# A linear-attention and expert-ffn layer on one core: the own-token term moved onto the diagonal of the attention matrix, the output gated from PSUM, a new order of the slot's tail

## What is computed

```python
x = x + _layernorm(attn(_layernorm(x)))
x = x + _layernorm(ffn(_layernorm(x)))
# attn: 4 heads, 64 key and 128 value features a head
S = jnp.exp(gt)[:, None] * S + kt[:, None] * vt[None, :]   # step over tokens
o = qt @ S
o = o * lax.rsqrt(mean(o * o, -1) + EPS) * rms_w           # per head
o = o.reshape(b, t, DV) * silu(x @ Wg)
return o @ Wo
# ffn: 8 experts, two sequences each
h = gelu(tokens @ w1 + b1); y = h @ w2 + b2
```

## Time and profile before

| | us |
|---|---|
| median of 3 runs | 1318.27 (1318.04 to 1319.22) |
| the profiled execution, its own time | 1316.67 |
| its span, first to last instruction | 1314.9 |
| TensorE busy | 1245.6 (95%) |
| VectorE busy | 1035.5 (79%) |
| ScalarE busy | 711.3 (54%) |
| GpSimd busy | 637.5 (48%) |

### The profile page before, as it was taken

One profiled execution on the slowest core, in us unless ns is written; L12 is line 12 of the kernel. 1 busy time (PEld: TensorE's weight loads), 2 busy tenths in 40 slices (PEclk: granted clock), 3 DMA queues, 4 the chain that ended last, 5 costly groups with the idle time before them and its releaser, 6 DMA issues. The chain is left out here.

```text
span 1314.9 us, 23430 instructions
## 1 busy us (share of the span) xinstructions
PE 1245.6 (95%) x8388; PEld 1096.4 (83%) x8388; DVE 1035.5 (79%) x2404; ACT 711.3 (54%) x1427; POOL 637.5 (48%) x889
## 2 busy tenths in 40 slices
PE   5889999999999999999999999999999999999957
PEld 3778889888898888889888888988889888898956
DVE  4769788796978969788787978879787796978863
ACT  5365555655456465654756555565545646465423
POOL 5436453563445544564435644356354554456431
PEclk9989999999999999999999999999999999999988
DMA  2110010100101001010011001010010100100000
GB/s 97 37 33 17 17 49 1 53 17 17 49 21 48 3 17 49 22 49 2 17 49 53 16 17 47 3 53 16 17 49 18 44 9 17 49 21 33 1 17 16
DMA packets 31778, 38.27 MB, mean 29 GB/s; under 512 B 2448, under 2 KB 29104, under 8 KB 31664
## 3 DMA queue, kind: packets, MB, share of 16 engines
q1 hardware_dynamic: 31136, 36.25, 8.3%
q10 hardware_dynamic: 528, 0.52, 0.1%
HBM read 28.38 MB, written 8.39 MB: 28 GB/s over the span
## 5 line engine op out<-in xcount | busy, mean ns | idle before, releaser
L1041 POOL TENSOR_TENSOR k_decayed<-k_decayed,block_totals 128x256 f32<-128x256 f32 x192 | 170.4, 887 | 248.3 <-PE ps_level L304 248.0
L304 PE MATMUL ps_level<-q_blockdiag,k_decayed 128*128 128x128 f32 x1792 | 263.9, 282 | 13.2 <-DVE q_blockdiag L586 12.5
L304 PEld LDWEIGHTS ps_level<-q_blockdiag,k_decayed 128*128 128x128 f32 x1792 | 234.9, 191 | 34.9 <-DVE q_blockdiag L586 24.6
L576 DVE COPY_PREDICATED attn_T<-level_masks,ps_level 128x512 f32<-128x512 uint32 x160 | 153.1, 957 | 21.6 <-PE ps_level L304 21.4
L1047 POOL TENSOR_TENSOR rstd<-rstd,minus_half 128x1 f32<-128x1 f32 x192 | 111.7, 584 | 106.5 <-DVE rstd L638 106.5
L586 DVE TENSOR_TENSOR q_blockdiag<-q_blockdiag,block_totals 128x512 f32<-128x512 f32 x192 | 140.0, 730 | 27.3 <-PE ps_level L304 27.2
L261 PE MATMUL ps_big<-w_ff_hi,h_hi 128*128 128x256 f32 x512 | 150.0, 293 | 2.5 <-DVE h_lo L591 2.5
L263 PE MATMUL ps_big<-w_ff_hi,h_lo 128*128 128x256 f32 x512 | 144.8, 283 | 0.0
L262 PE MATMUL ps_big<-w_ff_lo,h_hi 128*128 128x256 f32 x512 | 144.7, 283 | 0.0
L838 ACT ACTIVATE gelu_out<-ps_big,ff_b_cols 128x512 f32<-128x512 f32 x128 | 88.0, 688 | 80.2 <-PE ps_big L263 48.9
L624 DVE SCALAR_TENSOR_TENSOR o<-o,o_rstd,out_gate 128x128 f32<-128x128 f32 x256 | 93.3, 425 | 45.0 <-POOL o_rstd L1063 45.0
(11 more groups left out here) (110 smaller groups left out, 3203.1 us busy)
## 6 DMA issues: line engine op xcount, KB each, us to landing
w_raw<-L_ffn_w SPq DMA_DIRECT2D x16, 1024.0 KB, 5.5
out<-y SPq DMA_DIRECT2D x16, 512.0 KB, 2.9
x_in<-L_attn_x SPq DMA_DIRECT2D x15, 512.0 KB, 3.9
ff_b_rows<-L_ffn_b SPq DMA_DIRECT2D x8, 128.0 KB, 2.1
x_in<-L_attn_x ACTq DMA_DIRECT2D x1, 512.0 KB, 4.0
w_raw<-L_attn_Wv SPq DMA_DIRECT2D x1, 512.0 KB, 5.4
w_raw<-L_attn_Wg SPq DMA_DIRECT2D x1, 512.0 KB, 6.7
y<-L_attn_Wo SPq DMA_DIRECT2D x1, 512.0 KB, 7.7
```

What stands on the lines that cost most here:

```text
L304: last = nc.tensor.matmul(PL[tl][:, c * CH:(c + 1) * CH], kk[:, tl, c * CH:(c + 1) * CH], q[:, :, :, 1, :], start=True, stop=True)
L576: nc.vector.copy_predicated(dst, m.to_broadcast([P, 2 * NCH, HC // h, h]), src)\
L1041: nc.gpsimd.tensor_tensor(k, k, t.to_broadcast([P, T // (2 * h), h]), ALU.mult)\
```

## The change

Five things change.

1. `diag` leaves level 0. Behind level 0, `diag_rows` makes the sums as rows: 32 weight columns (`head_sum`, now with one block for each feature tile) against q times k, one strip of 32 PSUM partitions for each chunk. ScalarE copies them to SBUF, and after step 3 TensorE transposes them (`diag_columns`). VectorE copies the columns to `qk_diag` at step 4.
2. `diagonal(c)` puts them on the diagonal of `attn_T`: one masked copy for each chunk at steps 6 to 9, with the identity as mask. `att(c)` then holds the own-token term, and `o_part` is gone.
3. `squares` and `og` read PO itself. So `att(c + 1)` waits for `og(c)` instead of `o_part(c)`.
4. The tail is in a new order on all four engines. The fourth `wo` writes the bank of the state (`WOB`), and three of the four last projection tiles stand ahead of it.
5. The fourth chunk's transposes of k and the fourth chunk in the last `k_update` are left out, as no later chunk reads them. The waits of `own_wait` made no instruction here, since the slots are numbered by plain integers, and they are gone.

```diff
+        WOB = [PL[0], PL[1], PL[0], PS]
...
-                        if i == 0:
-                            self_product = diag(c, tl)
                     last.then_inc(sem["pe_lv"], 1)
...
+                def diag_rows():
+                    for tl in range(KT):
+                        for c in range(NCH):
+                            last = nc.tensor.matmul(PO[32 * c:32 * (c + 1), 0:CH], ind[:, tl, :],
+                                                    qk[:, tl, c * CH:(c + 1) * CH], start=(tl == 0), stop=(tl == KT - 1))
+                    last.then_inc(sem["pe_drow"], 1)
+                def diag_columns():
+                    pe.wait_ge(sem["ac_dg"], at("ac_dg", s, 1))
+                    nc.tensor.transpose(PO[:, CH:2 * CH], o[:, 0, 0:CH], ident[:, :]).then_inc(sem["pe_diag"], 1)
...
-                    for c in range(2):
+                    for c in range(2 - f):
...
-                        pe.wait_ge(sem["dv_o"], at("dv_o", s, c * H))
+                        pe.wait_ge(sem["dv_og"], at("dv_og", s, c * H))
                         pe.wait_ge(sem["dv_st"], at("dv_st", s, states(c)))
                     else:
-                        pe.wait_ge(sem["dv_dg"], at("dv_dg", s, 1))
+                        pe.wait_ge(sem["dv_dia"], at("dv_dia", s, NCH))
...
                         level(step // 2, step % 2)
+                        if step == 1:
+                            diag_rows()
+                        if step == 3:
+                            diag_columns()
...
-                def o_part(c):
...
+                def diagonal(c):
...
+                    dve.wait_ge(sem["dv_cp"], at("dv_cp", s, c + 7))
+                    blocks = Am[:, :, 2 * c:2 * c + 2, :]
+                    m = ident[:, :].bitcast(U32).rearrange("p (k a q) -> p k a q", k=1, a=1)
+                    d = dg[:, c * H:(c + 1) * H].rearrange("p (k a q) -> p k a q", k=KT, q=1)
+                    nc.vector.copy_predicated(blocks, m.to_broadcast([P, KT, 2, CH]), d.to_broadcast([P, KT, 2, CH]))\
+                        .then_inc(sem["dv_dia"], 1)
...
-                        nc.vector.scalar_tensor_tensor(o[:, c % 2, w], o[:, c % 2, w], rso[:, c * H + hd:c * H + hd + 1],
+                        nc.vector.scalar_tensor_tensor(o[:, c % 2, w], PO[:, w], rso[:, c * H + hd:c * H + hd + 1],
                                                        gs[:, c, w], ALU.mult, ALU.mult).then_inc(sem["dv_og"], 1)
...
                 def squares(c):
-                    act.wait_ge(sem["dv_o"], at("dv_o", s, H * (c + 1)))
+                    act.wait_ge(sem["pe_att"], at("pe_att", s, c + 1))
```

More of the change, by code:

```diff
@@ L430, in st @@
                     elif C:
-                        pe.wait_ge(sem["dv_st"], at("dv_st", p, states(NCH - 1)))
+                        pe.wait_ge(sem["dv_t"], at("dv_t", p, NCH))
                     for tl in range(KT):
@@ L473, in wo @@
                     pe.wait_ge(sem["dv_oglo"], at("dv_oglo", s, c + 1))
-                    if c >= 2:
-                        pe.wait_ge(sem["dv_t"], at("dv_t", s, c - 1))
-                    else:
-                        pe.wait_ge(sem["ac_cp"], at("ac_cp", s, 5 + c))
-                    three(PL[c % 2][:, 0:D], [(ogT_hi[:, k, :], ogT_lo[:, k, :]) for k in range(VT)],
+                    if c == 3:
+                        pe.wait_ge(sem["dv_st"], at("dv_st", s, states(NCH - 1)))
+                    elif c == 2:
+                        pe.wait_ge(sem["dv_t"], at("dv_t", s, 1))
+                    else:
+                        pe.wait_ge(sem["ac_cp"], at("ac_cp", s, 6))
+                    three(WOB[c][:, 0:D], [(ogT_hi[:, k, :], ogT_lo[:, k, :]) for k in range(VT)],
                           [(WO[0][:, k, :], WO[1][:, k, :]) for k in range(VT)]).then_inc(sem["pe_wo"], 1)
@@ L727, in run @@
                         q_update(step // 2, step % 2)
+                    if B and 6 <= step < 6 + NCH:
+                        diagonal(step - 6)
                     if C:
@@ L774, in run @@
                 if B:
+                    state(1)
                     og_lo(0)
                     og(1)
+                    ln2(0)
+                    normed_attn(0)
                     state(2)
-                    o_part(2)
-                    ln2(0)
                     og_lo(1)
-                    o_part(3)
                     og(2)
-                    normed_attn(0)
-                    ln2(1)
-                    og_lo(2)
-                    og(3)
-                    normed_attn(1)
                 if A:
@@ L790, in run @@
                 if B:
-                    og_lo(3)
+                    ln2(1)
+                    ln3_stats(0)
+                    og_lo(2)
+                    normed_attn(1)
                 if A:
@@ L797, in run @@
                 if B:
-                    ln3_stats(0)
+                    og(3)
+                    ln3(0, s)
                     ln2(2)
-                    ln2(3)
-                    ln3(0, s)
+                    og_lo(3)
                     ln3_stats(1)
                     normed_attn(2)
+                    ln3(1, s)
+                    ln2(3)
+                    ln3_stats(2)
                     normed_attn(3)
-                    ln3(1, s)
-                    ln3_stats(2)
+                    ln3(2, s)
                     ln3_stats(3)
-                    ln3(2, s)
             program(dve, run)
@@ L951, in run @@
                     og_hi(1)
-                    squares(3)
                 if A:
@@ L957, in run @@
                 if B:
+                    squares(3)
                     og_hi(2)
-                    og_hi(3)
                 if A:
@@ L998, in late_constants @@
                 fill(masks[:, :, :], 1.0)
-                fill(ind[:, :], QSCALE)
-                select(ind[:, 0:1], [[0, 1]], HK - 1, -1)
-                select(ind[:, 1:2], [[0, 1]], -HK, 1)
+                fill(ind[:, :, :], 0.0)
+                for tl in range(KT):
+                    pool.wait_ge(c_step, count[0])
+                    fill(ind[:, tl, 2 * tl:2 * tl + 2], QSCALE)
+                    select(ind[:, tl, 2 * tl:2 * tl + 1], [[0, 1]], HK - 1, -1)
+                    select(ind[:, tl, 2 * tl + 1:2 * tl + 2], [[0, 1]], -HK, 1)
                 for i in range(MASKED):
```

125 lines of the change are left out of this document (56 added, 69 removed).

## The result

| | before | changed |
|---|---|---|
| median, us | 1318.74 (1318.04 to 1319.48, 4 runs) | **1362.82** (1354.4 to 1367.1, 4 runs) |
| ratio, 95% interval | | 1.0322 (1.0295 to 1.0349): slower |
| profiled execution, its span | 1316.67, 1314.9 | 1354.4, 1352.7 |
| TensorE, VectorE busy | 95%, 79% | 92%, 73% |
| mean granted clock | 0.988 | 0.967 |

The forecast was 1356, with a range from 1327 to 1384. The next rows are the table by stretches of the changed kernel, for the same two slots as the earlier trace rows. From the top: a and b of the even slot, the tile behind wo(3), the rest of the seam, a and b of the odd slot, and the seam behind it in one row.

What follows compares the result with a forecast made beforehand. TensorE hardly pauses in stretches a and b, but VectorE times the seam c + d between slots. 60.6 - 33.8 + 10.2 + 2.3 = +39.3 on 1316.67 gives 1356 us, range 1327 to 1384.

Steps and rivals of the forecast that it cites:

- Stretch b: Gate matmuls to end of fourth wo: three tiles and new waits make it 35.4 us in both kinds of slot, +60.6.
- Stretch c: Fourth wo to VectorE's first masked copy of the next slot: a chain of 5.2 us against 7.45, -33.8 over 15 starts.
- Stretch d: First masked copy to level 2 of the next slot: VectorE in order, so it keeps 7.62 and 6.86 us.
- Stretch a: First matmul of level 2 to the gates: diagonal copies cost +0.4 even, +1.3 odd, less 0.2 for transposes; +10.2.
- first slot's levels: First attention slot, with no ffn to hide the diagonal copies: +2.5 - 0.2 = +2.3 us.
- last slot's tail: Last slot's tail, no projections between: chain as long as before, o_part shorter but att(c+1) waits for og(c); 0.
- two new waits: Before the fourth wo: vp(0) waits 0.4 for k's copy, ogt(3) 0 to 1.14 for og(3); together 0.5 taken.
- diag_rows: TensorE's row sums in the seam (c + d): taken as 1.6 us, covered by x3t's wait for ln3.
- Rival 1: Seam (c + d) closes, TensorE's own 9.0 us times the start: 1304; deciding point a 9.8 us seam; chance 0.08.
- Rivals 2 and 5: 2: diagonal copies cost 1.1 each, 1386, chance 0.09; 5: diag_rows at 0.45 a matmul, +11, 1367, chance 0.05.
- rival 3: Tail and levels absorb it: no new waits, free diagonals, seam 0.5 shorter; 1328; chance 0.71 together with the forecast.
- rival 4: Gains and losses cancel if og leaves earlier and the chain overlaps more: 1314 to 1319; chance 0.04.

Runs made afterwards that it cites:

- e3: Changed kernel with the eight products of diag_rows issued twice; 1356.89 us.
- e6: Changed kernel with GpSimd's split of the second ffn weight cut to 16 columns of each quarter for experts 1 to 7; 1341.29 us.
- e4: Changed kernel without the masked copies of levels 0 and 1 (each cut to two or four elements); 1337.60 us.
- e12: e9's kernel with unneeded TensorE work added: diag_rows four times over ahead of x3t, sixteen products of its kind behind x3t; 1370.18 us.
- e5: Changed kernel with the old tail order on all engines and the attention output copied out of PSUM by VectorE; 1327.57 us, ratio 1.0088.
- e1: Changed kernel with the fourth wo product one token tile earlier on TensorE, ahead of vp(3); 1351.82 us.
- e2: Changed kernel with the fourth wo product one token tile later on TensorE, behind gp(3); 1388.68 us.
- e8: The changed kernel again, word for word; 1356.35 us, ratio 1.0326.
- e9: Changed kernel with the four diagonal copies moved on VectorE from steps 6 to 9 to behind step 13; 1351.03 us.
- e10: e5's kernel with its diagonal copies moved behind the levels in the same way as e9; 1313.58 us, ratio 0.9964.

## Why the prediction held, step by step

The terms of the sum, against the two profiled executions (spans 1314.9 and 1352.7, so +37.8), added up over all slots:

| term | forecast | measured |
|---|---|---|
| b, 15 slots | +60.6 | +59.5 |
| c, 15 starts | -33.8 | -29.3 |
| d | 0 | +6.9 (14 starts) |
| a, steady slots | +10.2 (15 slots) | -7.4 (14 slots) |
| first slot's levels | +2.3 | +3.2 |
| last slot's tail | 0 | +4.2 |

These make 37.1; the rest lies in the lead-in and the last slot's levels. That the sum came within 2 us of this execution is in part luck: a is 17.6 below its forecast, and c, d, the first slot and the tail are 16.5 above theirs. In the second way to run (e3's profile) a is +12.0 and d -0.9 over 14 slots, near their forecasts: the prediction's account of the levels fits the second way, its total the first.

**Stretch b** came to 35.44 and 35.41 for 35.4. Its two new waits are there, with the sizes the other way round: vp(0) waits 0.23 for 0.4, and ogt(3) 0.51 where little of a group was taken.

```profile
564.16 0.50 PE L256 MATMUL ps_big<-w_vg_hi,xT_hi 128*128 128x512 f32 x1 [0.23 <-ACT k_decayed L832]
...
587.22 0.66 PE L464 MATMUL ps_transpose<-ident,o 128*128 128x128 f32 x4 [0.51 <-DVE o L626]
```

og never takes 2.1 for four now: the 256 instructions take 340 to 352 ns. The rule of the Trainium skill weighed there (VectorE: DVE Perf Modes, the TRN2 errata) does not show: from PSUM the middle one takes 344 ns, from SBUF it took 347.

**Stretch c** is 5.50 for 5.2, the same links. What is dearer is the last of them: ln3(3) takes 0.92 us where it took 0.41, and the masked copy follows 0.83 after its start instead of 0.3. It now runs beside GpSimd's first k updates, which followed it before; the other links together are 0.2 cheaper.

```profile
596.52 1.70 POOL L1049 TENSOR_TENSOR k_decayed<-k_decayed,gates 128x256 f32<-128x256 f32 x2
```

**Stretch d** was forecast unchanged and is 8.46 and 6.99 against 7.62 and 6.86. The step that failed is that VectorE alone sets it. In the odd slot the q update that level 2 needs ends 7.65 us after the masked copy, at 605.07, as the forecast has it:

```profile
603.95 1.12 DVE L586 TENSOR_TENSOR q_blockdiag<-q_blockdiag,block_totals 128x512 f32<-128x512 f32 x1
```

But behind TensorE's idle time f1(0) runs at the lower clock and ends at 605.88, and level 2 is queued behind it (last section). In even slots it is level 1 that runs at the lower clock; where the clock holds there (e3, e6), d is 6.55 to 6.58.

**Stretch a** has the right mechanism and a wrong size, by which way the slot runs. Even slots: the copies cost nothing (31.56 for 31.90), where I had +0.4. Odd slots: 34.09 where level 2 comes early (e3), +1.5 against 32.62 for a forecast of +1.1; but 31.65 where it comes late, as in the profiled execution. The median of four runs, 1362.8, lies between the two ways. That GpSimd can hold the diagonal copy (the Trainium skill, SBUF — State Buffer, "Who interferes with whom") agrees with a row of e3: 1.18 us for one beside k_update, 0.73 as a rule. By e6 it matters more for the q updates beside the split, 1.45 and 1.72 for 0.71.

**The last slot's tail**, priced at 0, is 36.16 from att(0) to x3t against 31.94. With no projections, every link of att, squares, root and og lies open; one row of TensorE's timeline shows it:

```profile
1286.20 0.77 PE L450 MATMUL ps_out<-v,attn_T 128*128 128x128 f32 x2 [2.68 <-DVE o L626]
```

**diag_rows** takes 0.64 and not 1.6; being covered (e3), the error cost nothing.

**Rival 1**, a closed seam, needed 9.8 us; it is 12.5 to 14.0. e4 shows why: with 4.4 us of VectorE's work gone it is still 10.3 to 11.3. Rivals 2 and 5 fall by the rows above (a copy takes 0.73, a product of diag_rows 0.08), rival 3 by 26 us or more and rival 4 by 35 or more.

## What to carry to other kernels

Before work is moved on the engine that bounds the kernel, ask what it covers where it stands: the seam was VectorE's, and three tiles taken out of it cost their full 4.25 us a slot while the chain beside them gave back 2. A shorter path that keeps a PSUM bank longer (squares and gating straight from it) can be the dearer one, together with the order that it asks for; a plain copy that frees the bank at once, on the engine that has time for it, in the old order, was 0.75% faster than the kernel before. And instructions that are free in one slot can cost 1.6 us in the next, where another engine's work slows their neighbours, so their place has to be looked up in each kind of slot.

## What the runs showed of the hardware

TensorE's clock fell behind its waits. The changed kernel's table by stretches, from the start of an odd slot: level 0 to x3t, x3t to level 1, level 1, f1(0) with one transpose ahead of it, and the next steps.

```profile
593.31:597.56 4.25, 2.55 (x34) 2.15 (x32) 3.27 (x9) 2.67 (x3) 3.09 (x6) 1.00 0.22 77
597.56:600.05 2.49, 1.10 (x9) 0.86 (x9) 2.49 (x3) 1.08 (x2) 1.88 (x2) 1.00 0.23 83
600.05:603.50 3.45, 2.89 (x17) 2.69 (x18) 3.45 (x5) 0.00 (x0) 2.20 (x2) 0.78 0.00 0
603.50:605.88 2.38, 2.38 (x8) 1.91 (x8) 2.38 (x3) 0.00 (x0) 2.16 (x3) 0.60 0.01 3
605.88:609.50 3.62, 3.62 (x25) 3.29 (x24) 3.00 (x6) 3.30 (x5) 2.82 (x4) 1.00 0.00 0
```

TensorE is busy 2.55 of 4.25 and 1.10 of 2.49 us; after that it is granted 0.78 and then 0.60, part of the time the lower of its two levels (1.2 of 2.4 GHz), and f1(0) takes 2.32 us where f1 takes 1.46 at 1.00. In the next row it is 1.00 again. With the gaps filled (e12) it never fell in a steady slot.

The same waits do not always bring a fall. e6 has both among its odd slots without the split, level 0 to x3t, x3t to level 1, and the next 2.25 us (first a slot without a fall, then one with it):

```profile
750.62:754.87 4.25, 2.58 (x34) 2.18 (x32) 3.27 (x9) 2.67 (x3) 3.08 (x6) 1.00 0.24 78
754.87:757.37 2.50, 1.83 (x14) 1.59 (x15) 2.50 (x3) 1.09 (x2) 0.81 (x2) 1.00 0.22 77
...
592.06:596.31 4.25, 2.55 (x34) 2.16 (x32) 3.27 (x9) 2.67 (x3) 3.09 (x6) 1.00 0.27 79
596.31:598.81 2.50, 1.83 (x12) 1.60 (x13) 2.50 (x3) 1.08 (x2) 0.84 (x2) 0.88 0.22 78
598.81:601.06 2.25, 2.25 (x12) 2.19 (x12) 2.25 (x5) 0.00 (x0) 0.92 (x2) 0.50 0.00 0
```

What decides it there is open. The same two slots show what a fall costs, start to level 2:

```profile
750.62:761.28 10.66, 7.68 (x64) 6.08 (x62) 9.68 (x17) 3.76 (x6) 6.03 (x11) 1.00 0.15 51
...
592.06:603.14 11.08, 8.71 (x64) 7.78 (x63) 10.10 (x17) 3.76 (x5) 6.08 (x10) 0.85 0.16 49
```

That is 0.42 us a start, and 0.3 to 0.4 a slot (79.43 against 79.03 to 79.13). In odd slots with the split a slot with a fall can be the cheaper one. e5 shows it inside one execution, in two odd slots, start to level 2 and then a:

```profile
588.31:597.89 9.58, 7.60 (x64) 6.09 (x63) 9.10 (x13) 3.93 (x6) 7.38 (x9) 1.00 0.16 56
597.89:632.12 34.23, 32.53 (x233) 29.70 (x233) 30.23 (x61) 15.35 (x25) 14.19 (x17) 1.00 0.00 1
...
745.90:756.47 10.57, 8.84 (x65) 7.57 (x64) 10.10 (x13) 3.76 (x5) 8.34 (x9) 0.84 0.16 50
756.47:788.12 31.65, 31.65 (x234) 29.82 (x232) 26.86 (x61) 15.29 (x25) 15.15 (x17) 1.00 0.01 2
```

The second of them, the only one of the seven whose clock fell, reaches level 2 1.0 us later and takes 78.56 us; the six others take 80.1.

Over the 43 steady odd slots that have the split and the copies in the steps (the changed kernel, e1, e2, e3, e5, e8, one of e6), a is 31.6 to 31.7 wherever level 2 starts 8.45 us or more after the first masked copy (17 slots), and 34.1 to 34.6 wherever it starts 8.43 or less after it (26 slots); e2 and e5 have both in one execution. So the two ways are ways of a slot, and the lateness of level 2 behind VectorE tells them apart. That it lets h_lo keep up is argued and not shown, and so is why the border is this sharp. With the copies moved behind the levels the two cost the same: from the masked copy to the gates it is 39.9 to 40.2 us in every steady odd slot of e9 and e10, early level 2 or late, against 40.1 to 40.5 (late) and 41.7 to 42.5 (early) with the copies in the steps. This fits e9, whose runs no longer fall into two groups.
